# Expert stage: the output product moved ahead of the transposes, and expert matrices loaded one by one

## The reference, cut to what matters

```
scores = softmax(xf @ Wg.T);  w, idx = top_k(scores, 2);  w = w / w.sum()
h1 = xf @ (W1 + B1 A1)^T + b1          # 256 -> 512, per expert
h3 = xf @ (W3 + B3 A3)^T + b3          # 256 -> 512
g  = silu(h1) * h3
y_e = g @ (W2 + B2 A2)^T + b2          # 512 -> 256
y  = sum over the 2 chosen experts of w_e * y_e
```

## Time and profile before

| | |
|---|---|
| median of 3 runs | 1159.03 us (1158.61 to 1160.38) |
| profiled execution | 1158.17 us, span 1156.5 us |
| mean granted clock of TensorE | 0.957 of full speed |
| PE busy | 1066.6 us, 92% |
| DVE busy | 786.2 us, 68% |
| ACT busy | 392.3 us, 34% |
| POOL busy | 427.5 us, 37% |
| expert stage, first to last PE work | about 639 to 1003 us of the span |

### The profile page before, as it was taken

The page is one execution under the profiler, slowest core; times in us unless marked ns, Lnnn a source line. Parts: engine busy times, 40 slices in busy tenths (PEclk is TensorE's granted clock), DMA queues, the critical chain, the costliest instruction groups (busy, mean ns, idle before and its releaser), DMA issues. The chain is left out here.

```text
span 1156.5 us, 20362 instructions
## 1 busy us (share of the span) xinstructions
PE 1066.6 (92%) x6338; PEld 921.1 (80%) x6338; DVE 786.2 (68%) x1743; ACT 392.3 (34%) x768; POOL 427.5 (37%) x408
## 2 busy tenths in 40 slices
PE   5999999999999993599994899999999989899996
PEld 4899999999998993477773688888888878777875
DVE  5688887887878673556764477777777757663755
ACT  3645554463646331242210222222222212342210
POOL 2846454463645430074474000000000000088875
PEclk8999999999999995699997899999999989899998
DMA  9354563675466238463573715152454241275554
GB/s 266 98 191 161 171 207 127 192 181 199 125 181 194 102 139 202 131 187 96 181 222 111 259 51 183 55 188 70 173 187 172 72 169 47 85 151 86 85 114 91
DMA packets 115475, 170.70 MB, mean 148 GB/s; under 512 B 17200, under 2 KB 89520, under 8 KB 115248
## 3 DMA queue, kind: packets, MB, share of 16 engines
q1 hardware_dynamic: 95408, 122.19, 34.5%
q0 software_dynamic: 19968, 47.23, 14.2%
HBM read 98.24 MB, written 71.14 MB: 146 GB/s over the span
## 5 line engine op out<-in xcount | busy, mean ns | idle before, releaser
L1714 PE MATMUL wide<-expert_ring,xsT 128*128 x852 | 232.5, 409 | 7.0 <-POOLq L1696 5.5
L1714 PEld LDWEIGHTS wide<-expert_ring,xsT 128*128 128x128 f32 x852 | 153.2, 192 | 35.3 <-issue 8.0
L1773 ACT ACTIVATE gsT<-bank 128x512 fp32r<-128x512 f32 x71 | 42.6, 600 | 255.7 <-PE bank L1733 255.7
L1601 POOL DMA_DIRECT2D expert_ring<-experts_scratch x24 | 17.0, 714 | 285.1 <-issue 285.1
L1714 PEld LDWEIGHTS bank<-expert_ring,gsT 128*128 128x128 f32 x852 | 111.8, 188 | 6.6 <-issue 0.3
L1714 PE MATMUL bank<-expert_ring,gsT 128*128 x852 | 113.8, 282 | 0.1
L1826 DVE TENSOR_TENSOR h<-wide,expert_bias 128x512 f32<-128x512 f32 x71 | 49.1, 692 | 81.5 <-PE wide L1714 80.6
L1256 POOL DMA_INDIRECT slot_rows_scratch<-ring,slot x64 | 67.7, 1057 | 69.1 <-DVE slot L1561 48.4
L1242 POOL DMA_INDIRECT first_half<-slot_results_scratch,slot x32 | 52.1, 1628 | 89.1 <-DMA first_half<-x_scratch 80.3
L444 POOL TENSOR_TENSOR folded_matrix<-fold,folded_matrix 128x512 fp32r<-128x512 f32 x48 | 63.9, 1339 | 39.8 <-ACT folded_matrix L636 37.0
L460 PE MATMUL wide<-xnT,w 128*128 128x512 f32 x234 | 60.5, 400 | 0.0
(11 more groups left out here) (279 smaller groups left out, 2407.0 us busy)
## 6 DMA issues: line engine op xcount, KB each, us to landing
experts_scratch<-folded_matrix SPq DMA_DIRECT2D x24, 1024.0 KB, 5.2
expert_ring<-experts_scratch POOLq DMA_DIRECT2D x24, 1024.0 KB, 7.4
raw<-in_expert_weights SPq DMA_DIRECT2D x24, 512.0 KB, 7.2
xs_ring<-slot_rows_scratch SPq DMA_DIRECT2D x71, 128.5 KB, 2.1
slot_results_scratch<-ys_ring SPq DMA_DIRECT2D x71, 128.0 KB, 2.1
slot_rows_scratch<-zeros SPq DMA_DIRECT2D x23, 385.5 KB, 7.1
ring<-xn_scratch SPq DMA_DIRECT2D x32, 257.0 KB, 3.3
xn_scratch<-xb SPq DMA_DIRECT2D x16, 512.0 KB, 7.3
```

Source lines behind the costliest of these rows:

```text
L1714: ins = mm(o, parts[i], moving, start=(first and q == 0), stop=(last and q == 2))
L1773: return nc.scalar.activation(o, i, ACT.Copy)
```

## The change

- PE and DVE: in turn j, `out_rows(j)` comes directly behind the W1 product of tile j+2 and ahead of `gated(j + 1)` and `rows(j + 3)`. The W3 product is last in the turn.
- The arrival of each matrix has a semaphore of its own (`expert_in[slot][m]`, `expert_ready[m]`). PE waits for m = 0 ahead of the W1 product, for m = 1 ahead of the W3 product, and for m = 2 ahead of the output product.
- For the experts from rank 2 on, W1 and W3 are asked for when `h_taken` says that the last tile of e-2 has passed its W3 product; W2 when `y_taken` says so, after W1 and W3 have arrived.
- The biases are loaded in two DMAs, b1 and b3 with W1, b2 with W2. LE:3 falls out of POOL's list of the attention stage.
- The ring of row tiles in SBUF has 6 places instead of 8.
- Some semaphores in `route` and `attention` on which nothing waits are dropped.

```diff
-        SC:26 SC:27 YS:9 LE:3 SC:28 YS:10 ...
+        SC:26 SC:27 YS:9 SC:28 YS:10 ...
...
 def load_expert_part(pool, io, keep, scr, j, m, e):
+    arrived, slot = keep["expert_in"][j % 2][m], j % 2
+    at = slice(2 * HID * m, 2 * HID * (m + 1))
+    pool.dma_start(keep["experts"][:, 1 - slot, :, at].bitcast(F32),
+                   scr["experts"][bass.ds(e, 1), :, :, at].rearrange("e p h n -> (e p) h n")).then_inc(arrived, 16)
+    if m != 1:
+        at = slice(0, 2 * HID) if m == 0 else slice(2 * HID, BIASES)
+        pool.dma_start(keep["expert_bias"][:, slot, at],
+                       io["expert_bias"][bass.ds(e, 1), at].to_broadcast([P, at.stop - at.start])).then_inc(arrived, 16)
+PARTS_IN = (32, 16, 32)
...
-    ROUND = 8
+    ROUND = 6
...
         def _(pool):
+            def arrived(e, m):
+                pool.wait_ge(keep["expert_in"][e % 2][m], PARTS_IN[m] * (e // 2 + 1))
+                pool.sem_inc(expert_ready[m], 1)
             for e in range(E):
-                if e == 1:
-                    load_expert(pool, io, keep, scr, e)
+                if e:
+                    of = expert_of_rank(pool, keep, e)
                 if e >= 2:
                     end = pool.value_load(keep["rank_end"][0:1, e - 2:e - 1], min_val=0, max_val=SLOTS_T)
+                    hold(pool, loader_held, h_taken, end + 2)
+                for m in (0, 1):
+                    if e:
+                        load_expert_part(pool, io, keep, scr, e, m, of)
+                if e < 2:
+                    if e:
+                        load_expert_part(pool, io, keep, scr, e, 2, of)
+                    for m in range(3):
+                        arrived(e, m)
+                else:
+                    for m in (0, 1):
+                        arrived(e, m)
                     hold(pool, loader_held, y_taken, end + 2)
-                    load_expert(pool, io, keep, scr, e)
-                pool.wait_ge(keep["expert_in"][e % 2], 64 * (e // 2 + 1))
-                pool.sem_inc(expert_ready, 1)
+                    load_expert_part(pool, io, keep, scr, e, 2, of)
+                    arrived(e, 2)
...
             def hidden(j, e, m):
-                    pe.wait_ge(expert_ready, e + 1)
+                pe.wait_ge(expert_ready[m], e + 1)
             def out_rows(j, e):
+                pe.wait_ge(expert_ready[2], e + 1)
...
             for j in range(SLOTS_T - 1):
                 if j + 2 < SLOTS_T:
                     hidden(j + 2, of[j + 2], 0)
+                out_rows(j, of[j])
                 gated(j + 1)
                 if j + 3 < SLOTS_T:
                     rows(j + 3)
                     of[j + 3] = expert(pe, j + 3)
                 if j + 2 < SLOTS_T:
                     hidden(j + 2, of[j + 2], 1)
-                out_rows(j, of[j])
```

More of the change, by code:

```diff
@@ L182, in build @@
             keep["expert_bias"] = sb("expert_bias", [P, 2, BIASES], F32, held)
-            keep["expert_in"] = [held.enter_context(nc.semaphore(f"expert_in{i}")) for i in range(2)]
+            keep["expert_in"] = [[held.enter_context(nc.semaphore(f"expert_in{i}_{m}")) for m in range(3)] for i in range(2)]
             attention(nc, io, keep, scr, psum, 0, out, at + ring)
@@ L915 @@
         SC:16 SC:17 YS:3 SC:18 SC:19 LE:0 LE:1 YS:4 YS:5 YS:6 YS:7 SC:20 LE:2 SC:21 SC:22 SC:23 SC:24 SC:25 YS:8
-        SC:26 SC:27 YS:9 LE:3 SC:28 YS:10 YS:11 YS:12 YS:13 SC:29 YS:14 SC:30 YS:15 SC:31
+        SC:26 SC:27 YS:9 SC:28 YS:10 YS:11 YS:12 YS:13 SC:29 YS:14 SC:30 YS:15 SC:31
     """,
@@ L982, in route @@
         w_in, c_in, row_in = sem("l1_weights_in"), sem("l1_cols_in"), sem("l1_rows_in")
-        spread_ready, rowprod, folded = sem("ln1_bias_spread"), sem("l1_bias_products"), sem("l1_folded")
+        spread_ready, rowprod = sem("ln1_bias_spread"), sem("l1_bias_products")
         high, split = sem("l1_weights_high"), sem("l1_weights_split")
@@ L1050, in _ @@
             dve.wait_ge(row_in, 48)
-            tt(bv[:], bv[:], S[0][:, 0:H1], ALU.add).then_inc(folded, 1)
-            tt(cols[:, 4:8], cols[:, 4:8], S[1][:, 0:EC], ALU.add).then_inc(folded, 1)
-            tt(cols[:, 8:10], cols[:, 8:10], S[1][:, 512:514], ALU.add).then_inc(folded, 1)
+            tt(bv[:], bv[:], S[0][:, 0:H1], ALU.add)
+            tt(cols[:, 4:8], cols[:, 4:8], S[1][:, 0:EC], ALU.add)
+            tt(cols[:, 8:10], cols[:, 8:10], S[1][:, 512:514], ALU.add)
             for p in range(2):
@@ L1154, in attention @@
         else:
-            chosen, counted, within_ready, slots_ready, ranks_ready = (
-                sem("experts_chosen"), sem("choices_counted"), sem("within_ready"), sem("slots_ready"), sem("ranks_ready"))
+            chosen, slots_ready, ranks_ready = sem("experts_chosen"), sem("slots_ready"), sem("ranks_ready")
             ring_in = [sem(f"ring_in{i}") for i in range(RINGS)]
@@ L1642, in moe @@
         assert nc.sbuf_base <= limit, (nc.sbuf_base, limit)
-        expert_ready, loader_held = sem("expert_ready"), keep["held"]["gpsimd"]
+        expert_ready, loader_held = [sem(f"expert_ready{m}") for m in range(3)], keep["held"]["gpsimd"]
         x_high, g_high = sem("slots_high_ready"), sem("gated_high_ready")
@@ L1761, in _ @@
                     rows(j + 3)
-                if j + 3 < SLOTS_T:
                     of[j + 3] = expert(pe, j + 3)
@@ L1823, in h1_bias @@
                 s = j
-                dve.wait_ge(expert_ready, e + 1)
+                dve.wait_ge(expert_ready[0], e + 1)
                 dve.wait_ge(h_done, 2 * s + 1)
```

## The result

The change makes the kernel slower: 1204.03 us median (1202.34 to 1205.47, 4 runs) against 1159.35 (1158.61 to 1160.38, 4 runs), ratio 1.0384, 95% interval 1.0366 to 1.0402. The forecast was 1218, range 1200 to 1232. The profiled execution took 1205.47 us, span 1203.8, 47.3 above the span of before.

What follows compares the result with a forecast made beforehand. PE bounds the expert stage, busy 275.00 of 275 us at full clock. Profiled 1158.17 + 65.3 (new wait) + 2.2 (stage end) - 8.3 (load stall) = 1217.4; with the median 0.86 higher, 1218 us, range 1200 to 1232.

Steps and rivals of the forecast that it cites:

- The mechanism: Expert-stage turn: W1 product follows the row transposes with only the W3 product between; `xsT` takes 1.71 us, cover is 1.48.
- X: PE's transposes of the rows of tile j+3 in turn j of the expert stage, put at 0.14 us.
- H0: PE's W1 product of tile j+2 in turn j, 6 products of 512 columns, put at 1.39 us.
- H1: PE's W3 product of tile j+2 in turn j of the expert stage, put at 1.48 us.
- the price of one turn: Wait on `xsT` ahead of the W1 product: 0.86 us lost plus 0.10 slower start, 0.96 a turn, 68 times, 65.3 us.
- The Trainium skill's rule: Ahead of the W1 product, the wait sits on a register instruction and blocks PE's sequencer; restart after `xsT` takes 0.62 us.
- The end of the stage: From the last W1 product to the last output product: 9.5 us instead of 7.3, so 2.2 us more, bounds 0 and 3.
- The loads: Matrices one by one: all land in time, expert 7's stall before tile 60 goes, -8.3 us, bounds -8.3 and -5.5.
- The costs put at nothing: Added register waits on `expert_ready`, ring of 6, split biases and dropped semaphores cost nothing; bound +0.6 for the biases.
- third rival: Expert stage: the clock falls too; a quarter of the turns at 1.2 GHz add 48 us, 1266 us, chance 0.06.
- A sign I described wrongly: Sign of being right: some 68 PE waits for `xsT` at DVE L1814, 0.75 to 0.9 us each.
- A sign of being wrong that came: Attention stages moving by more than 1 us would show the forecast wrong; outside the expert stage it expected no change.

Runs made afterwards that it cites:

- The turns of 5.588 and 6.343 us: Changed kernel with one register operation less, or a second load of the tile's rank, behind the wait on `xsT`: 1215.72 and 1271.17 us, one run each.
- loads-only version: Changed kernel with the order of before on PE and DVE; loads one by one, split biases and ring of 6 stay: 1147.57 us, ratio 0.991.
- order-only version: Kernel before with only `out_rows(j)` moved up on PE and DVE; loads, waits and ring of before: 1208.64 us, ratio 1.0425.

## Why the prediction was right

- **The mechanism held as written**: X to H0 has only H1 between, the chain ACT gated, ACT rows, DVE gated, DVE rows takes 1.71 us to H1's 1.48, and the wait meets every turn. The earlier trace rows had shown it once, at 0.75 us of idle time in a stage of 367.
- **The term that was too large is the price of one turn**: 0.96 forecast, 0.78 measured, so 53.0 us instead of 65.3. Its parts: `xsT` 1.71 behind H1, as forecast; the empty start of H0 0.1, as forecast; from `xsT` to H0 0.62 forecast and 0.46 measured. I took that from the first turn of the stage, a single case. In it 0.25 us pass between the start of the move and that of the next sequencer instruction; in the changed kernel it is 0.09 us. Its first turn is no exception: 0.46 us from `xsT` to H0 there too, and its 2.23 us from H1 to H0 come from a later `xsT`. So the excess is a pause in the sequencer and not a price of the pattern; why it is there stays open. The 0.16 us, times 68, are 10.9 of the 12.3 us by which this term was too large.
- **The range held by some luck at its lower end.** Its 0.75 a turn was a bracket that begins at a modelled end, not a price: the same bracket reads 0.53 in the changed kernel, where a turn costs 0.78. 1204 lies just above the 1202 worked out from it.
- **The Trainium skill's rule**: by "Sequencer-only Instruction" of "Perfetto Trace Analysis" in the Trainium skill, a wait on a sequencer instruction holds the sequencer, where a tensor instruction waits in a queue. The turns of 5.588 and 6.343 us agree with the first: work behind the wait isn't done ahead of it.
- **The end of the stage**: 2.2 forecast. H0(70) to the last y instruction is 1051.10 - 1040.13 = 10.97 us, before it was 1002.90 - 993.83 = 9.07: 1.9. The total came near because two errors cancel. The restart behind `gsT` was put at 0.6 us twice and is 0.14 us; and G(70) waits about 0.5 us for g behind O(69), which the sum left out. The kernel before had already shown the cheap restart, 0.13 us behind `gsT` at 1000.92:

```profile
1001.05 1.50 PEld L1714 LDWEIGHTS bank<-expert_ring,gsT 128*128 128x128 f32 x12 [0.26 <-issue]
```

- **The loads**: -8.3 forecast for the removed stall and a landing about 10 us after the first issue; POOL found the two parts landed 11.2 us after it (961.67 to 972.85), 10.5 us ahead of H0(60) at 983.33. Right, but the terms aren't independent. Under the new order the stall alone would have been 4.35 us. So of the 8.3 us, about half went with the order and half with the loads; the sum counts them once and comes out right.
- **The costs put at nothing**: added register waits (turn unchanged in the loads-only version, and in the new order not longer than without them) and the ring (turn unchanged; its part in the wait for matrices is open). The split biases and POOL's list were never run alone; the loads-only version, which has both, began its stage 1.4 us earlier than the kernel before, within the differences of the same code.
- **Sum by measured terms**: 68 x 0.78 + 1.9 - 8.3 = 46.6 us, and the stage grew by 46.5.
- **The clock** (third rival) was 1.00 from 656 to 1050 us, with PE idle 0.5 us in each 5.68; it was lower only in the first 16 us of the stage (0.69), as before the change (0.74 in the first 18).
- **A sign I described wrongly**: waits of 0.75 to 0.9 us in the profile. They are 0.5, since idle time there begins at a modelled end. Only the starts gave the right size.
- **A sign of being wrong that came**: attention stages that moved by more than 1 us. The stages ahead of the expert stage took 1.8 us more. Since the same code there differs by up to 2.7 us between executions, this sign was set too tight and says nothing against the mechanism.

## What to carry to other kernels

In a loop that one engine fills to 100%, an order is a set of distances between producers and users; before moving a step, list what lay between each pair and compare it with the chain through the other engines, last link included. A stall that the profile shows once, at the start of a loop where the pipeline isn't filled, shows what an order that makes this gap regular will wait for. Its size there is one sample: here it held a pause of 0.16 us that did not repeat. Where a wait can be late, what the sequencer does behind it (register arithmetic, loads of indices) is on the path.

## What the runs showed of the hardware

- A register load with the two sequencer instructions behind it costs 0.66 us of PE's time in each turn when it stands behind a late wait, and nothing with 1.44 us of products ahead of it. One register operation less is 0.09 us.
- From the end of DVE's write to PE's first product it is 0.46 us with four instructions of PE's sequencer between (0.36 with three, in the run with one less), and 0.14 us at `gsT` with one. With the wait on the weight load itself, at G(70), it is 0.05 us. The group behind the 0.46 us wait then takes 0.1 us more (1.50 us where it was 1.39).
- In the order-only version every third turn is 0.09 us longer, by a pause between two sequencer instructions behind the late wait; the changed kernel doesn't have it. The cause is open.
- Loading 3 MB and the biases (640 KB) with one wait took 14.6 us from release to use in the kernel before and 16.6 in the order-only version. The biases, issued last, landed last: in the kernel before, the packets of the matrices end at 939.5 us, those of the biases at 941.3.
